# Attention mask of each pair's second head added by VectorE, and some work of the ends and queues placed elsewhere

## What is computed

```python
q, k, v = heads(ln(x) @ Wq + bq), heads(ctx @ Wk + bk), heads(ctx @ Wv + bv)
scores = q @ k.T / sqrt(64)
scores = where(mask, -inf, scores)          # per row and context row
x = x + (softmax(scores) @ v) @ Wo + bo

h = ln(x).reshape(2048, 256)
p = softmax(h @ Wg); vals, idx = top_k(p, 2); cw = vals / (sum(vals) + 1e-9)   # scattered to 8 columns
y[e] = silu(h @ W1[e] + b1[e]) @ W2[e] + b2[e]                                  # F = 1024
x = x + sum_e cw[:, e] * y[e] + 0.1 * (silu(h @ Ws1 + bs1) @ Ws2 + bs2)
```

## Time and profile before the change

| | us |
|---|---|
| runs | 635.04, 635.07, 635.55 |
| median | 635.07 |
| the profiled execution, its own time | 631.55 |
| its span (first to last instruction) | 629.5 |
| PE busy | 604.8 (96%) |
| PEld busy | 536.4 (85%) |
| ACT busy | 372.5 (59%) |
| DVE busy | 360.9 (57%) |
| POOL busy | 324.8 (52%) |

### The profile page before, as it was taken

One profiled execution on the slowest core, in us unless ns is written; L12 is line 12 of the kernel. 1 busy time (PEld: TensorE's weight loads), 2 busy tenths in 40 slices (PEclk: granted clock), 3 DMA queues, 4 the chain that ended last, 5 costly groups with the idle time before them and its releaser, 6 DMA issues.

```text
span 629.5 us, 13319 instructions
## 1 busy us (share of the span) xinstructions
PE 604.8 (96%) x4711; PEld 536.4 (85%) x4711; DVE 360.9 (57%) x740; ACT 372.5 (59%) x1036; POOL 324.8 (52%) x347
## 2 busy tenths in 40 slices
PE   6999999999999999899999899999999999999995
PEld 5776797779776886687988789999999999999995
DVE  4676626762686446765897343755555646564632
ACT  4779508671678339747346264948484848484650
POOL 4976517874579439647251700137425653564443
PEclk9999999999999999999999989999999999999999
DMA  8521262356335444300424538996979997989441
GB/s 267 161 68 35 85 168 87 112 169 175 102 118 169 135 166 146 90 1 0 139 73 151 159 116 285 340 308 185 315 209 339 234 347 190 358 221 311 99 102 20
DMA packets 57582, 106.35 MB, mean 169 GB/s; under 512 B 8173, under 2 KB 30734, under 8 KB 55598
## 3 DMA queue, kind: packets, MB, share of 16 engines
q1 hardware_dynamic: 42094, 63.44, 31.8%
q10 hardware_dynamic: 7840, 32.30, 14.0%
q0 software_dynamic: 7584, 9.76, 8.2%
HBM read 80.24 MB, written 26.16 MB: 169 GB/s over the span
## 4 chain that ended last, share of the span: by engine, by line
PE 70%; ACT 11%; DVE 7%; POOL 5%; issue 4%; another core or an unknown queue 2%; POOLq 0%; ACTq 0%; DVEq 0%
ACT pr L1094 7%; PE bank_s L304 4%; PE bank_s L1584 4%; PE bank_t L306 4%; PE bank_t L305 4%; PE bank_t L304 4%; PE bank_s L306 4%; PE bank_s L305 4%; PE bank_q L304 4%; PE bank_m L304 4%; PE bank_q L306 4%; PE bank_q L305 3%; PE bank_m L305 3%; PE bank_m L306 3%; PE bank_k L305 3%
## 5 line engine op out<-in xcount | busy, mean ns | idle before, releaser
L1094 ACT ACTIVATE pr<-bank_s,nmax 128x120 f32<-128x120 f32 x256 | 88.5, 372 | 42.6 <-DVE nmax L674 42.2
L490 POOL TENSOR_TENSOR pr<-pr,rsum 128x480 f32<-128x480 f32 x64 | 62.8, 988 | 60.7 <-DVE rsum L678 60.2
L1006 DVE TENSOR_TENSOR hh_lo<-hbT,hh_hi 128x512 fp32r<-128x512 f32 x78 | 53.9, 692 | 67.1 <-ACT hh_hi L1224 55.7
L597 POOL TENSOR_TENSOR nop<-nop 128x1 f32<-128x1 f32 x39 | 21.6, 553 | 124.2 <-issue 62.7
L1221 ACT ACTIVATE hbT<-bank_s,b_col 128x256 f32<-128x256 f32 (+1 forms) x120 | 42.6, 421 | 67.1 <-issue 26.3
L598 POOL DMA_INDIRECT out_dram<-yw,xs x39 | 66.3, 1700 | 10.4 <-POOL nop L597 8.8
L575 POOL DMA_INDIRECT xs<-rows_d,sorted_i x39 | 43.2, 1107 | 45.2 <-issue 26.5
L1094 ACT ACTIVATION_READ_ACCUMULATOR pr<-bank_s,nmax 128x1 f32 x256 | 55.6, 217 | 0.0
L1224 ACT ACTIVATE hh_hi<-hbT 128x512 fp32r<-128x512 f32 x78 | 49.3, 632 | 2.5
L1073 ACT ACTIVATE qh<-bank_q,bias_t 128x512 f32<-128x512 f32 x32 | 22.6, 706 | 42.5 <-PE bank_q L306 42.5
L1182 ACT ACTIVATE xg<-bank_s,bias_t 128x512 f32<-128x512 f32 x32 | 22.0, 688 | 38.5 <-PE bank_s L306 22.9
(11 more groups left out here) (367 smaller groups left out, 2153.4 us busy)
## 6 DMA issues: line engine op xcount, KB each, us to landing
praw<-in_L_ffn_W SPq DMA_DIRECT2D x32, 256.0 KB, 2.9
w2s<-zg_hi SPq DMA_DIRECT2D x32, 256.0 KB, 3.6
w2s<-zg_lo SPq DMA_DIRECT2D x32, 256.0 KB, 3.9
aT_hi<-w2s SPq DMA_DIRECT2D x32, 256.0 KB
aT_lo<-w2s SPq DMA_DIRECT2D x32, 256.0 KB
w2n_hi<-w2s ACTq DMA_DIRECT2D x6, 1024.0 KB
w2n_lo<-w2s ACTq DMA_DIRECT2D x6, 1024.0 KB
wq_raw<-in_L_ffn_W ACTq DMA_DIRECT2D x5, 1024.0 KB
```

The source lines that it names most:

```text
L490: nc.gpsimd.tensor_tensor(pt, pt, rsum[:, n % 2, h, :].rearrange("p (t a) -> p t a", a=1).broadcast_to([P, GT, SK]), ALU.mult).then_inc(s[ ...
L1006: nc.vector.tensor_tensor(hh_lo[:, n % 2, u, :], hbT[:, i % 4, :], hh_hi[:, n % 2, u, :].bitcast(F32), ALU.subtract).then_inc(s["hh_lo_s"], 1)
L1094: last = nc.scalar.activation(pr[:, n % 2, h, t, :], bank_s[h][:, t * SK:(t + 1) * SK], ACT.Exp, bias=nmax[st], accum_out=ssum[st])
```

## The change

1. The mask of the second head (h == 1) is no longer a product. DVE adds `maskb` to the raw scores from `bank_s1` into `pr[..., 1]`, takes the maxima there, and ACT exponentiates `pr[..., 1]` in place.
2. POOL's loads of `bo` and `bs2` come behind `rsqrt(0)`; DVE's `normalize` comes ahead of `c_turned(0)`.
3. The four parts of `wo` are split at pairs 1 to 4; `W2_AT` takes none at 2 and 3, and one each at 5 and 6.
4. Pair 29 holds only `query(31)`, pair 30 holds `key(31)`, and DVE's `k_out(31)` comes behind `pt_out(29)`.
5. Eight tiles are gathered at first, not fifteen; behind slot n's scatters follow the tiles 8 places on, not 15.
6. For the last slot DVE makes b2 x gate ahead, and adds bank x gate in one step out of PSUM.
7. PE waits for `hh_lo` unit by unit within the products, and behind the two register loads.

The core of the diff:

```diff
-        W2_AT = [{0: 0, 1: 0, 4: 0, 5: 0, 6: 0, 12: 2, 20: 2, 26: 2}.get(...)
+        W2_AT = [{0: 0, 1: 0, 2: 0, 3: 0, 4: 0, 12: 2, 20: 2, 26: 2}.get(...)
+        AHEAD = 8
...
-                for q in range(XU):
+                for q in range(AHEAD):
                     gather(q)
...
-                    for q in range(XU, NBLK):
-                        if SLOT_OF[q - XU] == n - 1:
-                            gather(q)
+                    for q in range(TILE0[n] + AHEAD, min(TILE0[n + 1] + AHEAD, NBLK)):
+                        gather(q)
...
                     for h in range(2):
                         sc = bank_s[h][:, 0:GT * SK].rearrange("p (t k) -> p t k", t=GT)
+                        if h == 1:
+                            dve.wait_ge(s["mb"], n // PAIRS + 1)
+                            if n >= 2:
+                                dve.wait_ge(s["tp"], 2 * (n - 2) + 2)
+                            nc.vector.tensor_tensor(pr[:, n % 2, 1, :, :], sc, maskb[:, :, :], ALU.add).then_inc(s["ms"], 1)
+                            dve.wait_ge(s["ms"], n + 1)
+                            sc = pr[:, n % 2, 1, :, :]
                         nc.vector.tensor_reduce(nmax[:, n % 2, h, :], sc, AX.X, ALU.max, negate=True).then_inc(s["mx"], 1)
...
-                        if n:
+                        if n and h == 0:
                             pe.wait_ge(s["ex"], 2 * (n - 1) + h + 1)
-                        nc.tensor.matmul(bank_s[h][:, 0:GT * SK], identb[:, :], maskb[:, :, :], start=True, stop=False)
+                        if n and h == 1:
+                            pe.wait_ge(s["ms"], n)
+                        if h == 0:
+                            nc.tensor.matmul(bank_s[h][:, 0:GT * SK], identb[:, :], maskb[:, :, :], start=True, stop=False)
...
-                                                    kh[r, n % 2, b * SK:(b + 1) * SK], start=False, stop=t == GT - 1)
+                                                    kh[r, n % 2, b * SK:(b + 1) * SK], start=h == 1, stop=h == 1 or t == GT - 1)
...
+                    if n == NS - 1:
+                        for q in range(TILE0[n], TILE0[n + 1]):
+                            dve.wait_ge(s["yw_s"], q - 1)
+                            nc.vector.tensor_scalar(yb[:, q % 2, :], b2_e, gate(q), None, ALU.mult).then_inc(s["yadd"], 1)
...
+                            nc.vector.scalar_tensor_tensor(out=yw[:, q % YW, :], in0=bank_y[q % 3][:, 0:C], scalar=gate(q), in1=yb[:, q % 2, :],
+                                                           op0=ALU.mult, op1=ALU.add).then_inc(s["yw_s"], 1)
...
                 def expert_down(n):
                     wide, j = SEQ[n]
-                    pe.wait_ge(s["hh_lo_s"], UNIT0[n + 1])
                     if wide:
...
                             for f in range(NF):
+                                if t == 0 and f % 2 == 0:
+                                    pe.wait_ge(s["hh_lo_s"], UNIT0[n] + f // 2 + 1)
```

46 lines of the change are left out of this document (29 added, 17 removed).

## The result

The changed kernel takes **638.24 us** (median of 20 runs, 633.94 to 640.83), the kernel before 635.11 in the same series (20 runs, 634.40 to 636.12): a ratio of **1.0039 (1.0028 to 1.0050)**, slower by 0.4%, where -0.5% was forecast. The medians lie 3.1 us apart, the ratio gives 2.5. The profiled execution has a span of 637.3 us against 629.5. The runs of the changed kernel spread over 7 us, those of before over 2.

The account below looks back on a forecast made before the run. TensorE, busy 604.8 of 629.5 us, was taken as the bound. Terms -0.4 - 0.3 - 5.1 + 4.0 - 1.65 = -3.45 took the profiled 631.55 to 628.1; with 3.52 carried over, 631.6 us, range 626.5 to 637.5.

Parts of the forecast that it names:

- The ring of the plain pair: Attention: VectorE's chain from one attend to the next, with the new add, takes 5.68 us against 5.69.
- the plain pairs, some 24 of 32: Attention: count of plain pairs, which would lose 0.17 us each if the add cost 0.86.
- -0.4 for mask and moves together: Attention: mask edit and moved steps together were to give -0.4 us, bounds -1 and +4.5.
- its walk through the 32 pairs: Attention: following three queues, attend was to start 0.07 to 1.2 us earlier, 0.4 at the end.
- The 6.7 us "on offer": Attention: TensorE's work saved over 32 pairs by dropping one mask product; forecast as offered, but handed back almost in full.
- the price of issuing late, +4.0: Expert stage: TensorE waits for late gathered rows at slot 4, with lower clock; +4.0 us, bounds 0 and 10.
- rival (d): Expert stage: rows late at slots 4 and 10, +9.8 us in place of +4.0, giving 637.4 us; chance 0.20.
- elsewhere the gathers are issued at least 6 us ahead of the reader: Expert stage: apart from slots 4 and 10, gathers were to have at least 6 us before TensorE reads.
- The stall, -5.1: Shared FFN: ScalarE's and VectorE's standstill during fifteen gathers was to go with eight, 3.4 us wait plus 1.7 clock.
- the 3.52 us between profile and median: Whole kernel: the runs' median of 635.07 us lies 3.52 above the profiled execution; carried over to the forecast.
- The end, -1.65: Last slot: TensorE's wait goes (-1.1 us) and the last tile's two VectorE steps become one (0.57 less); bounds -0.5, -1.7.
- The start, -0.3: Start: earlier xrows and row loads off the identity's path were to save between 0 and 0.6 us.

Follow-up runs that it names:

- masked_twice: Kernel before with VectorE's mask add for the second head beside TensorE's kept mask product: 642.12 us against 635.02, ratio 1.0110.
- second_unmasked: Kernel before with neither mask product nor add for the second head: 633.77 us against 635.02, ratio 0.9975.
- b_moves: Kernel before with only the moved wo and W2 pieces and key(31): 628.68 us against 630.37, ratio 0.9966.
- b_mask: Kernel before with only the second head's mask added by VectorE: 631.46 us against 626.28, ratio 1.0079.
- b_gathers8: Kernel before with only the gathers changed, eight tiles at first and lookahead 8: 637.15 us against 626.28, ratio 1.0177.
- a_masks_on_pe: Changed kernel with both mask products back on TensorE: 636.37 us where the kernel before takes 626.28, ratio 1.0139.
- lookahead12: Kernel before with eight gathers at first, six behind slot 0's scatters, then lookahead 12: 630.46 us against 635.04, ratio 0.9926.
- two_batches: Kernel before with its first fifteen gathers split, eight first and seven once slot 0's rows are turned: 627.75 us against 635.02, ratio 0.9890.
- b_end: Kernel before with only the last slot's output step and the unit-by-unit hh_lo waits: 628.82 us against 630.37, ratio 0.9974.
- b_start: Kernel before with only the bo and bs2 loads and the normalize step reordered: 635.04 us against 635.04, ratio 0.9999.

## Why the prediction was wrong

**The ring of the plain pair was right.** 5.68 us, the add 0.65, its own wait 0.03 and the first maximum at 2.53 were all measured as forecast; masked_twice and second_unmasked (5.89 and 5.47) confirm the ring from either side. What failed is the count of pairs that it holds for, and the prices of two other terms.

**One step that failed is "the plain pairs, some 24 of 32".** The term of the sum was -0.4 for mask and moves together; measured are +2.2 between the first and last `attend` of the two traces. The mask alone costs 3.8 there at the full clock, the moves alone bring 1.4, and 3.8 - 1.4 = 2.4. In the trace of before only six of the 31 distances between `attend`s are the 5.68 or 5.69 of the plain pair. Where VectorE also has layer-norm statistics, residuals or the gate, it works from `a_lo` to the copies without a gap, and what the add costs varies: four distances are 0.6 to 0.8 us longer in the changed kernel (those to pairs 9, 17, 25 and 29), several 0.1 to 0.4, and some others give back 0.15 to 0.35. The forecast named these pairs ("would lose up to 0.68 each, less what the earlier scores and the slack before them give"), but its walk through the 32 pairs let every `attend` start earlier than before. In the trace every one starts later, by up to 2.8 us. The moves' gains are there: at the last `attend` b_moves is 1.4 us ahead of before, counted from the first, and at the one before it the changed kernel 1.6 ahead of b_mask. The loss beside them was what the walk had too small. The 6.7 us "on offer" was wrong as well; second_unmasked shows 1.8 at the last `attend` and 1.3 by the runs.

**The step that was furthest off is the price of issuing late, +4.0.** Its mechanism was right, and it is rival (d), put at 0.20. The size was off by nearly three: 10.9 us in b_gathers8, 12.3 in the profile. Of the forecast places slot 4 is late in every trace with a lookahead of 8. Slot 10 is late in a_masks_on_pe (3.07 us, against 3.2 forecast), but not in this profile, where slots 14 and 16 are, nor in b_gathers8, where slots 11 and 17 are. The time from issue to use differs from trace to trace: for tile 8 it is 7.6, 8.1, 8.7 and 9.5 us in b_gathers8, lookahead12, the changed kernel and a_masks_on_pe. The sentence "elsewhere the gathers are issued at least 6 us ahead of the reader" took 6 us for enough, while the earlier trace rows itself showed 9.89 for scatters. And the forecast priced what follows a wait only by a lower clock, not by the register loads of a wide slot's products: the waits at slots 4 and 16 cost 1.96 + 1.25 + 1.7 = 4.9 us and 1.83 + 1.16 + 1.6 = 4.6, that at slot 14 only its own 2.1. As to the fit of the Trainium skill's page "DMA: Bandwidth & Descriptors", section "Anatomy of one DMA — SWDGE (gpsimd) path", which gives an estimated 2.3 us for such a gather: in this stage the trace does not agree; tile 8's gather is issued at 408.38, and TensorE gets its rows at 417.10, 8.7 us later.

**The stall, -5.1, was right in kind, with its condition.** The two traces show -5.5, and the runs -7.3 (two_batches), on chips that have it; on the chip of the first series it is 0. Twelve gathers in place of fifteen give 2.0 us by the runs. The size was low because the profile of before is of an execution of 631.55 us, below all twenty runs of before (634.40 to 636.12). The four profiles with fifteen gathers at 635 show a pause of 14.73 to 14.86 us in place of 11.75, and a stall of 8.2 to 9.4 us. The forecast carried the 3.52 us between profile and median over unchanged, although most of them are this stall and went with it.

The rule of the Trainium skill's page "DMA: Bandwidth & Descriptors", section "Queues, rings and completion order", that an engine for transfers takes turns between its queues, spoke for a stall that stays; the runs speak against using it here: fewer gathers end the stall, whatever the link is.

**The end, -1.65, was right**: -1.6 in b_end, -1.5 in the profile, although the single step lasts 0.48 and not 0.42. **The start, -0.3, was nothing**: with the row loads out of the way, TensorE began at 2.09, only to wait 1.70 for the context, and the first query started at 12.46 instead of 12.13.

With the measured terms the sum comes out near the result: -7.3 (stall, by the runs of two_batches) + 10.9 (rows) + 2.2 (mask and moves) - 1.6 (end) = +4.2; with 8.5 for the stall, by the stretch in b_start, it is +3.0. Measured are +2.5 to +3.1. The terms come from different chips, and late rows let single runs differ by 7 us, so the closer fit is in part luck. That the forecast missed its range by only 0.7 us is luck too: the rows alone were 6.9 us above their term, the attention 2.6, and the larger stall took back 3.4 of it.

## What to carry to other kernels

Before work is moved off the busiest engine, run the kernel once with that work left out for free: here it would have said that 1.3 to 1.8 of the 6.7 us can be had, before the add is paid for. Where a queue's latency varies from run to run, count the distance between issue and use in terms of the worst row of that queue, and look at what stands behind a wait in TensorE's queue: waits of about 2 us cost 2.1 to 4.9 us here, by whether register loads and a lower clock followed. Before the step at one place is put down to the edit, look at the granted clock there: 1.6 of the 5.4 us of b_mask were the clock. And compare the profile's own time with the runs, since here a profile below all of them showed less of the wait that was to be removed. Of a change in seven parts, running them apart showed two that cost (the mask, and the gathers, whose price is paid back in part where before has the stall), one that does nothing (the start) and two groups that gain; these two with ten gathers at first gave 1.2% less than before.

## What the runs showed of the hardware

ScalarE's exponentials started closer together when they read PSUM and wrote SBUF than when they read and wrote the same SBUF tile. The first head's exponentials (128x120, with the row sum) start every 0.33 us, the second head's, which now read and write the same SBUF tile, every 0.38; four of each in a row:

```profile
39.80 0.35 ACT L1115 ACTIVATE pr<-bank_s,nmax 128x120 f32<-128x120 f32 x1
40.13 0.36 ACT L1115 ACTIVATE pr<-bank_s,nmax 128x120 f32<-128x120 f32 x1
...
41.18 0.40 ACT L1115 ACTIVATE pr<-pr,nmax 128x120 f32<-128x120 f32 x1
41.56 0.39 ACT L1115 ACTIVATE pr<-pr,nmax 128x120 f32<-128x120 f32 x1
```

That is 0.2 us more per pair, where the forecast had taken ScalarE's pitch to stay as it is; the plain pair stays at 5.68 all the same. Whether the source or the shared tile is the reason was not tried. The kernel before takes 626.3, 630.4 or 635.0 us in series on different chips, and on the last kind 7.3 us of this go with seven gathers moved elsewhere: one stall of ScalarE and VectorE beside a stream of gathers on POOL's queue.

TensorE's granted clock fell to 0.50 (1.2 of 2.4 GHz) behind a single wait of 1.98 us with products right up to it and right behind it (b_gathers8, at 556 us, for 558 to 560), and stayed at 1.00 behind waits of 2.12 us (the changed kernel, at 526) and 2.41 us (a_masks_on_pe, at 560). Of the ten late rows in the four traces six were followed by a lower clock. What decides it, these traces don't tell.
